# Sign-weight loads issued by GpSimd, keys stored in one row, new instruction orders: a post-norm decoder layer on one core

## The reference

```python
x = layernorm(x + attention(x, Wq, bq, Wk, bk, Wv, bv, Wo, bo))   # 16 heads of 32, causal
q, k = ctx @ Wxq.T + bxq, ctx @ Wxk.T + bxk                        # 128 wide
x = layernorm(x + x @ softmax(q @ k.T).T)                          # xattn, no scale
xq = quantise(rms_norm(x))                                         # whole numbers, 127 steps a row
h = silu(xq @ sign(W_g).T) * (xq @ sign(W_u).T)                    # 2048 wide
x = layernorm(x + h @ sign(W_d).T)
```

## Time and profile before

| | before |
|---|---|
| three timed runs | 584.73, 582.45, 584.68 us, median 584.68 |
| profiled execution | 582.25 us, its span 580.5 us |
| PE busy | 551.1 us (95%), 5506 matmuls |
| DVE busy | 480.5 us (83%) |
| ACT busy | 426.7 us (74%) |
| POOL busy | 371.8 us (64%) |
| granted TensorE clock, mean | 0.996 |

### The profile page before, as it was taken

The page is one execution under the profiler, slowest core; times in us unless marked ns, Lnnn a source line. Parts: engine busy times, 40 slices in busy tenths (PEclk is TensorE's granted clock), DMA queues, the critical chain, the costliest instruction groups (busy, mean ns, idle before and its releaser), DMA issues. The chain is left out here.

```text
span 580.5 us, 14560 instructions
## 1 busy us (share of the span) xinstructions
PE 551.1 (95%) x5506; PEld 359.4 (62%) x5506; DVE 480.5 (83%) x1258; ACT 426.7 (74%) x801; POOL 371.8 (64%) x403
## 2 busy tenths in 40 slices
...
GB/s 305 309 239 163 112 270 211 197 49 104 126 166 128 110 110 212 167 166 97 74 110 163 193 172 74 126 192 85 44 123 161 143 183 188 127 110 37 23 32 36
DMA packets 210597, 81.82 MB, mean 141 GB/s; under 512 B 197088, under 2 KB 201696, under 8 KB 208992
## 3 DMA queue, kind: packets, MB, share of 16 engines
...
## 5 line engine op out<-in xcount | busy, mean ns | idle before, releaser
L1276 POOL TENSOR_TENSOR ph<-p,ph 128x768 f16<-128x768 f32 (+1 forms) x78 | 141.5, 1822 | 50.3 <-ACT ph L847 35.6
L911 ACT ACTIVATE p<-ps_b,tops 128x128 f32<-128x128 f32 (+3 forms) x256 | 123.2, 552 | 26.4 <-DVE tops L1087 12.6
L1087 DVE CUSTOM_DVE_ANT_0 ps_b<-ps_b,future 128x128 f32<-128x128 f32 (+3 forms) x256 | 117.7, 521 | 8.4 <-PE ps_b L722 8.3
L814 PE MATMUL ps_b<-xqT,sg 128*128 128x256 f16 x1024 | 118.3, 272 | 3.5 <-ACT invb L847 1.7
L829 PE MATMUL ps_b<-sd,hp 128*128 128x512 fp8e4 x512 | 116.5, 379 | 0.0
L814 PEld LDWEIGHTS ps_b<-xqT,sg 128*128 128x128 fp8e4 x1024 | 98.5, 98 | 20.4 <-ACT sd L874 1.8
L1272 POOL TENSOR_TENSOR hp<-gt,hp 128x512 f16<-128x512 f32 x64 | 73.9, 1161 | 46.3 <-ACT hp L847 46.1
L665 PE MATMUL ps_b<-xhl,wh 128*128 128x256 f16 x480 | 82.9, 273 | 1.8 <-ACT p L911 1.6
L829 PEld LDWEIGHTS ps_b<-sd,hp 128*128 128x128 f16 x512 | 48.8, 98 | 56.0 <-issue 2.0
L847 ACT ACTIVATE ph<-p 128x768 f16<-128x768 f32 (+1 forms) x72 | 66.2, 926 | 8.1 <-DMA pt<-ph 7.8
L665 PE MATMUL ps_b<-xhl,wl 128*128 128x256 f16 x240 | 65.4, 273 | 0.0
(11 more groups left out here) (116 smaller groups left out, 951.1 us busy)
## 6 DMA issues: line engine op xcount, KB each, us to landing
hp<-in_sgT_dram SPq DMA_DIRECT2D x6, 1024.0 KB, 7.5
gt<-in_sgT_dram SPq DMA_DIRECT2D x6, 1024.0 KB, 6.6
...
out_dram<-rows SPq DMA_DIRECT2D x16, 256.0 KB, 2.5
xin<-in_xT_dram SPq DMA_DIRECT2D x14, 256.0 KB, 3.1
...
pt<-ph SPq DMA_TRANSPOSE x78, 4.3
hp<-in_wT_dram SPq DMA_DIRECT2D x4, 256.0 KB, 4.3
```

What stands on the lines that cost most here:

```text
L814: ins = pe.matmul(ps[:, a * HALF:(a + 1) * HALF], sg[:, ("gg", "uu").index(name), c, ht * P:(ht + 1) * P], xqT[:, c, :], start=c == 0, sto ...
L911: ins = act.activation(p32[:, n % P32_SLOTS, to:to + keys], ps[:, col:col + keys], ACT.Exp, scale=-1.0, bias=tops[:, s % 2, g, j, qt % 2:q ...
L1087: ins = dve.tensor_tensor_reduce(scores, scores, future[:, S - width:S], EXP_SCALE, 3e38, ALU.add, ALU.min, tops[:, s % 2, g, j, qt % 2:qt ...
L1276: pool.tensor_tensor(out_, in_, hi, ALU.subtract).then_inc(signal, 1)
```

## The change

The twelve `lg` steps leave SP's order and enter POOL's: `pool.dma_start` with the same waits, the same bytes and the same semaphores. POOL issued no DMA before. The keys lie in one row for each group and half, `ks[P, NG, 2, K_SLOTS * HALF]`, so that 384 neighbouring keys are one matmul too. All five orders are new; the multiset of steps on PE, ACT and DVE is the same, the banks of PE's products are dealt out anew.

```diff
 def key_runs(s, width):
-    if width == S and (s - 1) % K_SLOTS + 1 < K_SLOTS:
-        return ((0, S),)
+    if width > HALF and (s - 1) % K_SLOTS + 1 < K_SLOTS:
+        return ((0, width),)
     return ((0, min(width, HALF)), *(((1, width - HALF),) if width > HALF else ()))
...
 SP_ORDER = """
-lw0.0 lw0.1 lw0.3 lw0.2 lw2.0 lw1.1 lw1.3 lw2.1 lw1.0 bi lw1.2 lw2.2 sm lc0 lw3 lw2.3 lx1 lg0 lg1 lr0 lr1 lg2 lx2 lg3
...
+lw0.0 lw0.1 lw0.3 lw0.2 lw2.0 lw1.1 lw1.3 lw2.1 lw1.0 bi lw1.2 sm lc0 lw2.2 lw3 lw2.3 lx1 lr0 lr1 lx2 ta0.0 ta0.1
...
 POOL_ORDER = """
-k0 kb cs0.0 cs0.1 xs0.1.0 xs0.1.1 rb0.0.0 rb0.0.1 rb0.1.0 rb0.1.1 ta0.0 ta0.1 ta0.2 to0.0.0 to0.0.1 ta0.3 xs1.0.0
...
+k0 lg0 kb lg1 cs0.0 cs0.1 lg2 lg3 xs0.1.0 xs0.1.1 rb0.0.0 rb0.0.1 rb0.1.0 rb0.1.1 ta0.0 lg4 ta0.1 ta0.2 lg5 to0.0.0
+to0.0.1 ta0.3 lg6 xs1.0.0 xs1.0.1 tx0.0.0 os0.0.0 os0.0.1 lg7 lo0.1.1.0.1 lg8 tx0.0.1 xm0.0.0 n10.0.0 lg9 lo0.1.1.1.1
+lo0.1.2.0.1 lg10 lg11 xm0.0.1 n10.0.1 lo0.1.2.1.1 lo0.1.3.0.1 lo0.1.3.1.1 hh0.0.0 hh0.0.1 hh0.0.2 hh0.0.3 hh0.0.4
...
-        ks = sb("ks", [P, K_SLOTS, NG, 2, HALF], F16)
+        ks = sb("ks", [P, NG, 2, K_SLOTS * HALF], F16)
...
-            def load_signs(i):
-                if i < 2:
-                    sp.wait_ge(w_lo, 4 * (i + 1))
-                else:
-                    sp.wait_ge(signs, i - 1)
-                sp.dma_start(stage[i % 2], sgT[i]).then_inc(weight_in[i % 2], 16)
...
-                            slot, halves = (s - h + kh) % K_SLOTS, max(keys // HALF, 1)
+                            at = (s - h + kh) % K_SLOTS * HALF
                             for j in range(HG):
                                 mine = slice(DH * j, DH * (j + 1))
-                                scores = banks[j][:, col + kh * HALF:col + kh * HALF + keys]
-                                ins = pe.matmul(scores.rearrange("p (h n) -> p h n", h=halves),
+                                ins = pe.matmul(banks[j][:, col + kh * HALF:col + kh * HALF + keys],
                                                 qs[mine, s % Q_SLOTS, g, hq, qt % 2 * P:(qt % 2 + 1) * P],
-                                                ks[mine, slot:slot + halves, g, hk, 0:keys // halves],
+                                                ks[mine, g, hk, at:at + keys],
                                                 start=first, stop=last, skip_group_check=True)
...
+            def load_signs(i):
+                if i < 2:
+                    pool.wait_ge(w_lo, 4 * (i + 1))
+                else:
+                    pool.wait_ge(signs, i - 1)
+                pool.dma_start(stage[i % 2], sgT[i]).then_inc(weight_in[i % 2], 16)
```

More of the change, by code:

```diff
@@ L113 @@
+tq3.0.1 zn2.1.0 zn2.1.1 to3.1.0 to3.1.1 lr7 tx3.1.0 tx3.1.1 tq3.1.0 tq3.1.1 zn3.0.0 zn3.0.1 zn3.1.0 zn3.1.1
 """
 PE_ORDER = """
[L116 to L134, removed]
@@ new lines @@
+qk0.1.0@4 tw0.0.2.0.0@2,1 mx0.0.3.0@5,6,3,7 en0.3@4 tw0.0.2.0.1@2,0 qk0.1.1@1 tw0.0.3.0.0@2,6 pv0.0.2.0@3 pv0.0.2.1@3
+pv0.0.2.2@3 tw0.0.3.0.1@7,0 qk0.1.2@5 pv0.0.2.3@3 mx0.1.0.0@0,4,7,1 pv0.0.3.0@6 pv0.0.3.1@6 pv0.0.3.2@6 pv0.0.3.3@6
+qk0.1.3@2 tw0.1.0.0.0@7,3 mx0.1.0.1@1,5,4,0 tw0.1.0.0.1@7,6 mx0.1.1.0@6,7,1,3 tw0.1.0.1.0@4,5 op0.0.0@2 op0.0.1@0
+tw0.1.0.1.1@1,7 tw0.1.1.0.0@3,2 qk1.0.0@4 pv0.1.0.0@7 pv0.1.0.1@7 mx0.1.1.1@1,5,0,6 pv0.1.0.2@7 pv0.1.0.3@7 xm0.0.0@2
+tw0.1.1.1.0@7,5 mx0.1.2.0@0,1,4,3 qk1.0.1@6 qk1.0.2@5 qk1.0.3@4 tw0.1.2.0.0@3,6 mx0.1.2.1@1,0,7,2 xm0.0.1@5
@@ new lines @@
+mx1.0.2.0@2,3,6,0 va1.1.0@5 dn0.0.1.3@4 mx1.0.3.0@6,3,2,7 xm0.1.0@0 xm0.1.1@5 qk1.1.1@3 qk1.1.0@7 qk1.1.2@5 cp1.0@7
+cp1.1@2 ib1@3 pv1.0.0.0@0 pv1.0.0.1@0 pv1.0.0.2@0 mx1.1.0.0@5,6,4,1 pv1.0.0.3@0 pv1.0.1.0@2 pv1.0.1.1@2 pv1.0.1.2@2
+en1.0@7 en1.1@3 gg0.1.2@5 en1.2@4 gg0.1.1@6 pv1.0.1.3@2 gg0.1.0@0 uu0.1.0@7 en1.3@1 va1.1.1@3 uu0.1.1@0 uu0.1.3@2
+uu0.1.2@6 uu0.1.4@0 gg0.1.5@1 gg0.1.4@4 pv1.0.2.0@3 pv1.0.2.1@3 pv1.0.2.2@3 pv1.0.2.3@3 gg0.1.3@5 dn0.1.0.0@6
+pv1.0.3.0@7 pv1.0.3.1@7 pv1.0.3.2@7 pv1.0.3.3@7 gg0.1.7@3 uu0.1.7@5 uu0.1.5@2 qk1.1.3@7 gg0.1.6@0 uu0.1.6@1
@@ L167 @@
+xm3.1.0@0 xm3.1.1@4 dn3.0.0.0@0 dn3.0.0.1@0 dn3.0.0.2@0 dn3.0.1.2@2 dn3.0.1.3@2 dn3.0.0.3@0 ib7@4 gg3.1.0@1 gg3.1.6@0
+gg3.1.1@4 uu3.1.3@3 uu3.1.0@2 uu3.1.1@6 gg3.1.2@1 gg3.1.3@2 uu3.1.2@4 gg3.1.7@6 uu3.1.7@7 dn3.1.0.0@5 gg3.1.4@4
+gg3.1.5@2 uu3.1.4@3 uu3.1.5@1 dn3.1.0.1@5 uu3.1.6@4 dn3.1.1.0@2 dn3.1.1.1@2 dn3.1.0.2@5 dn3.1.1.2@2 dn3.1.0.3@5
+dn3.1.1.3@2
 """
 ACT_ORDER = """
-lx0 ws0.0 xs0.0.0 xs0.0.1 ws0.1 ws0.2 ws0.3 ws1.0 ws1.1 ws1.2 ws1.3 ws2.0 ws2.1 ws2.2 bv qk0.0.0 cs0.0 cs0.1 qk0.0.1
-wx qk0.0.2 qk0.0.3 ws2.3 ws3 ex0.0.0.0 ex0.0.0.1 ex0.0.0.2 cp0.0 cp0.1 va0.0.0 sg0 va0.0.1 hi0.0.0.0.0 ex0.0.0.3
@@ new lines @@
+cs0.1 qk0.0.2 qk0.0.3 ws2.3 ws3 cp0.0 cp0.1 ex0.0.0.0 ex0.0.0.1 ex0.0.0.2 va0.0.0 sg0 va0.0.1 hi0.0.0.0.0 sg1 xs0.1.0
+xs0.1.1 ex0.0.0.3 ex0.0.1.0 ex0.0.1.1 ex0.0.1.2 ex0.0.1.3 hi0.0.0.0.1 en0.0 en0.1 ez0.0 va0.1.0 ta0.0 hi0.0.1.0.0
+hi0.0.1.0.1 ov0.0.0 sg2 va0.1.1 ez0.1 en0.2 ex0.0.2.0 ov0.0.1 ex0.0.2.1 ex0.0.2.2 qk0.1.0 hi0.0.2.0.0 ex0.0.2.3 ta0.1
+ez0.2 hi0.0.2.0.1 ex0.0.3.0 ex0.0.3.1 ex0.0.3.2 ex0.0.3.3 hi0.0.3.0.0 qk0.1.1 hi0.0.3.0.1 en0.3 ta0.2 sg3 ov0.0.2
+qk0.1.2 ex0.1.0.0 ex0.1.0.1 ex0.1.0.2 ov0.0.3 ez0.3 ex0.1.0.3 hi0.1.0.0.0 to0.0.0 to0.0.1 ta0.3 hi0.1.0.0.1 ex0.1.0.4
@@ new lines @@
+qk0.1.3 ex0.1.0.5 ex0.1.0.6 sg4 ex0.1.0.7 xs1.0.0 ex0.1.1.0 xs1.0.1 ex0.1.1.1 tx0.0.0 ex0.1.1.2 ex0.1.1.3 hi0.1.0.1.0
+hi0.1.0.1.1 sg5 hi0.1.1.0.0 qk1.0.0 sg6 ov0.1.0 tx0.0.1 ex0.1.1.4 ex0.1.1.5 ex0.1.1.6 ex0.1.1.7 hi0.1.1.1.0 sg7
+n10.0.0 ex0.1.2.0 qk1.0.1 ex0.1.2.1 ex0.1.2.2 ex0.1.2.3 qk1.0.2 sg8 qk1.0.3 hi0.1.2.0.0 ex0.1.2.4 sg9 ex0.1.2.5
+ex0.1.2.6 ov0.1.1 ex0.1.2.7 hi0.1.2.1.0 n10.0.1 ex0.1.3.0 ex0.1.3.1 sg10 ex0.1.3.2 ex0.1.3.3 hi0.1.3.0.0 sg11 ib0
+ex0.1.3.4 ex0.1.3.5 ex0.1.3.6 ex0.1.3.7 ga0.0.0 ga0.0.1 hh0.0.0 ov0.1.2 hi0.1.3.1.0 hh0.0.1 ga0.0.2 ga0.0.3 hh0.0.2
```

331 lines of the change are left out of this document (163 added, 168 removed).

## The result

The change makes the kernel slower by 5.7%: 618.04 us median of 6 runs (613.98 to 621.43) against 584.01 of 6 (582.45 to 584.73), a ratio of 1.0573 with a 95% interval of 1.0543 to 1.0602. The prediction of 582.7 us, with a range up to 588.3, was wrong by 35 us. The profiled execution took 619.45 us, its span 617.3. PE is busy for 561.6 us of that, 10.5 more than before with 144 matmuls fewer, at a mean granted clock of 0.970 against 0.996; the other 26 us of the longer span are idle time.

The account below looks back on a forecast made before the run. PE, busy 551.1 of 580.5 us, was taken as the bound. Terms 0 + 0 + 1.3 - 2.4 - 0.9 = -2.0 us gave 582.7 us against the median 584.68, range 577.0 to 588.3.

Parts of the forecast that it names:

- (2): Early loads cost nearly nothing and later gaps close: -6.9 us or half, 579.4 as its middle; chance 0.36 with better-closing orders.
- (1): Early loads delay PE and ACT alike, nothing absorbs it, slow clock at 67 stays: +3.2 us, 587.9; chance 0.24.
- Keys in one row: Score products: 144 matmuls fewer but no fewer columns, so price 0; bound -2.3 us.
- Issuing on POOL: Twelve sign-load issues on POOL at 1.5 us each, 18 us of queue time, hidden: 0, with 1 us to the bad.
- The first two sign loads: At the start, `lg0` and `lg1` share bandwidth with the cross weights and delay them: +5.0 us on PE, +3.5 on ACT.
- the half that was taken: Early loads beside SP's weights: POOL's queue assumed to get half of 400 GB/s, so 1 MB takes 5.2 us.
- two thirds: Early loads: POOL's share by an alternative estimate from 8 KB sign rows against 2 KB weight rows.
- the 1.3 us: Extra on the early-load term if POOL's queue got that larger share instead of half.
- The gap at 67: PE's wait for ACT's exponentials is mostly absorbed by ACT's smaller lateness: -2.2 us, and -1.5 for the clock.
- Ahead of the feed-forward part: Before the first gate product, exponentials start sooner and `lg10` goes earlier, making signs ready 3 us sooner: -2.4 us.
- rival (3): Between 80 and 100 us full DMA engines make late sign loads land as late; the 2.4 fail: +0.4, 585.1; chance 0.15.
- The rest: At 177 `ib1` has another bank, half the freed time taken: -0.9 us; later gaps 0, 3 us to either side.

Follow-up runs that it names:

- orders_clean: Changed kernel's orders and key row, all sign loads issued by SP, `lg7` and `lg8` behind the transposes of their time; 598.30 us, ratio 1.0217.
- after_late_on_sync: Changed kernel with sign loads 5 to 11 back on SP, `lg0` to `lg4` still on POOL; 601.38 us, ratio 1.0267.
- key_row_alone: Kernel before with only the keys laid out in one row; 583.56 us, ratio 1.0010.
- orders_mended: orders_clean with three copies of queries and keys moved ahead of a row quantisation in DVE's order; 591.26 us, ratio 1.0132.
- late_in_small_rows: Changed kernel with sign loads 5 to 11 each cut into four quarter-row loads, still on POOL; 605.25 us, ratio 1.0379.
- late_on_pool: Kernel before with only the last seven sign loads (5 to 11) moved to POOL; 584.36 us, ratio 1.0011.

## Why the prediction was wrong, step by step

**The sum of what was lost.** By the ratios: orders 2.2%, first loads 0.5%, slow loads and transposes 3.1%; 12.7 + 2.9 + 17.9 = 33.5, the whole of 1.0573. The ratios of `orders_clean` and `after_late_on_sync` differ by less than their intervals, so the 3 us for the first loads are uncertain by as much. (The range's ends, 577.0 and 588.3, are not quite what rivals (2) and (1) add up to, 577.8 and 587.9; that changes nothing here.)

**Keys in one row, 0.** Right, as `key_row_alone` shows, and for its reason: 144 matmuls fewer, the busy time the same.

**Issuing on POOL, 0.** 1.5 us an issue was too high (0.53 to 0.76); but the cost of a POOL order isn't the issue, it is the wait in front of it. The prediction named `lg11` and `xm0.0.1`, and missed `lg3` and the input's low half; the changed kernel escapes it by ACT's order.

**The first two sign loads, +5.0 on PE.** The size came out near, the mechanism did not. The cross weights came no later. The timeline of ACT after:

```profile
14.23 1.28 ACT L859 ACTIVATE xqT<-ones,bv 128x128 f16<-128x128 f16 x4 [0.92 <-DMA scaled<-in_wxT_dram]
...
24.90 0.63 ACT L840 ACTIVATE wh<-o 128x512 f16<-128x512 f32 x1 [3.25 <-DMA o<-in_wT_dram]
```

ACT waited 0.92 us at `bv` and not 3.5, and it waits the same 0.92 in `orders_clean`, which has no load on GpSimd's queue: there `bv` only stands earlier. What failed is the start of the sharing. POOL issued `lg0` at 9.79, but its first packet went at 14.0, just as the cross weights had landed. From then on the sharing was stronger than the half that was taken: from 14 to 18 us (DMA view) POOL's queue moved 1.11 MB, SP's 0.60. (The prediction's two thirds came from packets of 8 KB against 2 KB, which would make four fifths, and the 1.3 us doesn't follow from either; nothing in its sum rests on them.) The first score product came at 20.29 and not 22.5, and PEclk was 1.00 up to 40 us, where a stretch of 0.5 near 24 was expected. The delay falls on the last weights: the prediction followed the one load with no slack and left out the ones behind it. Of the 4.5 us lost at 67, `orders_clean` has 1.0 as well (68.20); that the 3.5 left are the prediction's figure without its clock is luck.

**The gap at 67, -3.7 with its clock.** Not absorbed: 2.21 us are left, PEclk was 0.77 in the first microsecond behind it (the 12 products took 0.96 us) and 0.50 in the next two. It now waits for the low halves of a transpose on DVE, not for the exponentials on ACT, so ACT's lead bought nothing.

**Ahead of the feed-forward part, -2.4, and rival (3).** This step failed most. The first gate product was to come 1 us earlier and came 23 later. Rival (3) had the place and the partner, a sign load sharing with the transposes between 80 and 100 us, but priced it as landing as late as before. What happened is that both take two to four times as long, one transpose seven times: +18 for this step, where the forecast had -2.4 and rival (3) had 0. The prediction had the saturated windows in hand and counted only the loads' arrival, not the transposes', for which PE waits.

**The rest, -0.9 and 0 (3 to either side).** The second step that failed. The new orders cost 13 us, shown by `orders_clean`. At `ib1` there are 1.93 us of wait and not a gain. The prediction saw that `ib1` had another bank, but not who fills that bank just before and where DVE copies it out; it is the same at `xm0.0.1` and ahead of step 6's projections. Three such places and their slow clock were worth 5 us net. The remaining 8 us of the orders weren't traced to single words. In the profiled executions PE is busy 3.1 us longer in `orders_mended` than before (554.2 against 551.1), and stands still for the rest; and the prediction had no term for DVE's steps, which take up to five times as long beside POOL's.

**What stays open.** Why GpSimd's queue and SP's transposes get into the slow stretch under the new orders and not under those of before, with the same loads at nearly the same times, isn't settled. The Trainium skill (SBUF — State Buffer, Who interferes with whom) has GpSimd's descriptor writing held up by DVE. By that rule the loads could be slow, and ACT's queue free of it; it says nothing of transposes issued by SP, and no run here separates it. Also open is whether the packet size or the changed times made `late_in_small_rows` cheaper.

No kernel tried beats the one before; the best, `key_row_alone` and `late_on_pool`, equal it.
